# Feed-forward weight rounding moved from the first cross-attention's scores to its keys and values, read from a turned copy

## What is computed

```
# block 1: keys and values of context and latents, 4 kv heads of 96, 16 query heads
hidden = concatenate([context, latents], axis=1)          # 4096 + 256 tokens
k = hidden @ Wk.T ; v = hidden @ Wv.T ; q = latents @ Wq.T
out = softmax(q @ k.T / sqrt(96)) @ v @ Wo.T
# block 6: feed-forward in whole numbers, I = 2752, D = 1024
def _quant_w(W):                       # one scale for each row of W
    ws = maximum(max(abs(W), axis=1, keepdims=True) / 127, 1e-8)
    return clip(round(W / ws), -127, 127), ws
gate = (q @ Wgq.T) * s * wsg.T ; up = (q @ Wuq.T) * s * wsu.T     # Wg, Wu: 2752 x 1024
h = silu(gate) * up ; q2, s2 = _quant_act(h)
out = (q2 @ Wdq.T) * s2 * wsd.T                                   # Wd: 1024 x 2752
```

## Time and profile before

| | |
|---|---|
| median of 3 runs | 2087.39 us (2087.0 to 2088.69) |
| the profiled execution's own time | 2098.17 us |
| its span | 2096.8 us, mean granted TensorE clock 0.962 |
| latent stage, chunks 0 to 16 | 79.1 to 650 us |
| a context chunk of it | 33.9 us |
| cross stage, first score to the first matmul of its output projection | 659.94 to 1094.56 us |
| feed-forward stage | 2003 us to the end |

### The profile page before, as it was taken

How to read it: one execution, slowest core, us unless ns; L and a number is a source line. 1 busy time by engine, 2 the same in 40 slices (tenths; PEclk the granted TensorE clock), 3 DMA queues, 4 the chain that set the end, 5 groups by cost and what they waited for, 6 DMA issues and landing times.

```text
span 2096.8 us, 29638 instructions
## 1 busy us (share of the span) xinstructions
PE 1927.6 (92%) x11932; PEld 1414.5 (67%) x11932; DVE 1292.1 (62%) x1608; ACT 860.1 (41%) x1409; POOL 546.6 (26%) x264
## 2 busy tenths in 40 slices
PE   7899999999997999999998996989999999978977
PEld 5799999999996778787776874623333333366833
DVE  3445454454444788889976755757777774266465
ACT  2211111111113666665664451146777777535421
POOL 0000000000001555564510001046777777410000
PEclk9999999999998999999999998879999999999889
DMA  5543433343326656666625426523434320135052
GB/s 178 169 119 94 126 98 113 99 124 92 86 76 169 212 189 199 189 204 207 223 89 152 161 72 180 112 75 79 99 79 91 87 59 1 41 121 219 1 190 74
DMA packets 154808, 259.30 MB, mean 124 GB/s; under 512 B 36477, under 2 KB 102321, under 8 KB 147505
## 3 DMA queue, kind: packets, MB, share of 16 engines
q1 hardware_dynamic: 154673, 257.42, 41.3%
HBM read 192.39 MB, written 61.76 MB: 121 GB/s over the span
## 4 chain that ended last, share of the span: by engine, by line
PE 81%; DVE 10%; ACT 3%; DMA 2%; issue 2%; SPq 0%; POOL 0%; ACTq 0%; DVEq 0%
PE psum L475 10%; PE psum L1720 7%; PE psum L1737 5%; PE psum L456 4%; PE psum L458 4%; PE psum L457 4%; PE psum L443 3%; PE psum L285 3%; PE psum L286 3%; PE psum L287 3%; PE psum L1753 3%; PE psum L816 3%; DVE top L1913 3%; PE psum L817 3%; PE psum L818 3%; PE psum L831 3%
## 5 line engine op out<-in xcount | busy, mean ns | idle before, releaser
L1913 DVE TENSOR_REDUCE top<-psum 128x4 f32<-128x2048 f32 (+1 forms) x146 | 294.0, 2026 | 103.2 <-PE psum L1701 102.9
L1983 POOL TENSOR_TENSOR added<-probs_f 128x1024 f32<-128x1024 f32 x126 | 299.1, 2376 | 181.5 <-ACT probs_f L1838 133.7
L1838 ACT ACTIVATE probs_f<-psum 128x512 f32<-128x512 f32 x512 | 278.5, 594 | 142.0 <-PE psum L1720 129.7
L608 DVE TENSOR_REDUCE top<-psum 128x2 f32<-128x512 f32 x272 | 186.5, 692 | 198.0 <-PE psum L443 197.8
L907 DVE TENSOR_TENSOR probs_low<-probs,probs_high 128x1024 fp32r<-128x1024 f32 x136 | 197.7, 1458 | 77.7 <-ACT probs L870 77.5
L869 ACT ACTIVATE probs_high<-psum 128x1024 fp32r<-128x1024 f32 x136 | 139.9, 1029 | 164.1 <-PE psum L818 151.6
L1720 PE MATMUL psum<-q_rows,k_rows 97*128 97x512 f32 x512 | 197.7, 462 | 3.1 <-DMA q_rows<-t_high 2.4
L1720 PEld LDWEIGHTS psum<-q_rows,k_rows 97*128 97x128 f32 x512 | 80.9, 191 | 174.1 <-ACT probs_f L1838 159.0
L456 PE MATMUL psum<-c_high,w_high 128*128 128x256 f32 (+1 forms) x672 | 190.7, 284 | 3.2 <-issue 3.2
L457 PE MATMUL psum<-c_low,w_high 128*128 128x256 f32 (+1 forms) x672 | 190.6, 284 | 0.0
L458 PE MATMUL psum<-c_high,w_low 128*128 128x256 f32 (+1 forms) x672 | 190.5, 284 | 0.0
(11 more groups left out here) (359 smaller groups left out, 3820.2 us busy)
## 6 DMA issues: line engine op xcount, KB each, us to landing
wf_rows<-in_ffn_w_dram SPq DMA_DIRECT2D x42, 512.0 KB, 4.4
staged<-in_ctxT_dram SPq DMA_DIRECT2D x32, 512.0 KB, 4.7
k_four<-k_high SPq DMA_DIRECT2D x128, 128.0 KB, 3.4
wf_rows<-in_ffn_w_dram SPq DMA_DIRECT2D x8, 1376.0 KB, 7.9
q_dram<-wf_turned SPq DMA_DIRECT2D x42, 256.0 KB, 2.3
gate_up<-q_dram SPq DMA_DIRECT2D x10, 1024.0 KB, 8.1
value_high<-v_high SPq DMA_DIRECT2D x32, 256.0 KB, 3.7
value_low<-v_low SPq DMA_DIRECT2D x32, 256.0 KB, 4.6
```

The lines of the kernel that those rows point to most:

```text
L608: dve.tensor_reduce(top0[:, r0:r0 + 2, n], psum[:, bank, :].rearrange("p (i n) -> p i n", i=2), AX_X, ALU.max).then_inc(*b.bank_read.up())
L1838: act.activation(probs[:, n % 6, half * BANK:(half + 1) * BANK], psum[:, half, :], ACT.Exp, scale=scale).then_inc(*f.exped.up())
L1913: dve.tensor_reduce(top1[:, first:end, t, chunk], psum[:, MAXIMA + first:MAXIMA + end, :], AX_X, ALU.max).then_inc(*f.max_read.up())
L1983: pool.tensor_tensor(added[pair % 4][:], probs[:, n % 6, :], probs[:, (n + 1) % 6, :], ALU.add).then_inc(*f.added.up())
```

## The change

The rounding leaves the cross stage. It is done in chunks 1 to 15 of the latent stage, in six slots a chunk, 90 in all. A slot is one "find" step and one "settle" step, put between the steps of `chunk_steps` at places that the table `SLOTS` gives.

- The weights are read twice. The row maximum is found from rows as before (68 tiles `wf_rows` of 128 x 1024, three buffers; Wd in three parts). The values that are rounded come from a copy of the weights laid out transposed by the host (`ffn_t0` to `ffn_t2`), in 70 pieces ("pairs") of 128 x 2 x 512, four buffers `turned` (one tile of its own, `staged[2]`, and two halves of `xnT`). So PE turns nothing.
- The inverse scale now varies along the free dimension. SP writes a block's inverses to DRAM (`send_inverses`) and reads them back to all partitions (`load_inverses`). POOL multiplies a piece by them (TENSOR_TENSOR, 128 x 1024), ACT adds 12582912.0 and takes it away again into bf16 (two ACTIVATE of 128 x 1024, `settle`), SP stores the piece (`spill`).
- In slot i the "find" step finds tile i's maximum (DVE) and spills piece i - 18 (SP). The "settle" step rounds piece i - 17 (ACT), loads tile i + 3's rows and piece i - 15 (SP); the piece's buffer was spilled from at the "find" step one and a half slots before. SP waits for `topped`, `rounded` and `spilled` at these places.
- To free room, the low part of the queries is written into chunk 1's `c_high` and `c_low`, sent to DRAM and loaded again before the last chunk; ACT waits for `q_low_sent` before it splits chunk 1. The latents go to DRAM too and come back as a staged chunk. The context uses two `staged` tiles instead of four, and four loads stand ahead of the chunks instead of six.
- The cross stage keeps scores, exponentials, splits, `weigh` and `normalise`. The four unit splits stand at steps 120, 124, 128 and 132.
- The rounded weights lie in DRAM as the feed-forward stage's tiles have them: a partition's part of a chunk is 8 KB in one piece, before it was four of 2 KB. The matmuls of the last chunk (192 columns) take one pass instead of two.

```
+            SLOTS = {("mm", 0, 0, 0): "find", ("mm", 0, 0, 5): "settle", ("mm", 0, 1, 1): "find",
+                     ("mm", 1, 0, 0): "settle", ("mm", 1, 1, 0): "find", ("mm", 2, 0, 0): "settle",
...
             def act_chunk(n, half):
                 high = c_high[n % 2][:, 4 * half:4 * half + 4, :]
+                if n == 1:
+                    act.wait_ge(*b.q_low_sent.at(32))
...
+                def settle(r):
+                    z = width_of(*pairs[r][1:3])
+                    wide = turned[r % 4][:, 0:2 * z]
+                    act.wait_ge(*b.scaled.at(r + 1))
+                    act.activation(wide, wide, ACT.Copy, bias=ROUND).then_inc(*b.shifted.up())
+                    act.wait_ge(*b.shifted.at(r + 1))
+                    act.activation(turned[r % 4].bitcast(BF16)[:, 0:2 * z], wide, ACT.Copy,
+                                   bias=-ROUND).then_inc(*b.rounded.up())
...
+                    if m == 0:
+                        pool.wait_ge(*b.inverse_in.at(16 * (block + 1)))
+                    pool.wait_ge(*wt_in[r % 4].at(16 * (r // 4 + 1)))
+                    pool.tensor_tensor(both, both, inverses[block % 2][:, 0:width].unsqueeze(1).broadcast_to([P, 2, width]),
+                                       ALU.mult).then_inc(*b.scaled.up())
...
+                def load_rows(m):
+                    if m >= 3:
+                        sp.wait_ge(*b.topped.at(m - 2))
...
+                def load_turned(r):
+                    if r >= 4:
+                        sp.wait_ge(*spilled[r % 4].at(16 * (r // 4)))
...
+                    for i, part in enumerate(q_low_parts):
+                        sp.wait_ge(*b.q_split.at(8 * i + 8))
+                        sp.dma_start(q_low_dram[:, i * 8 * T:(i + 1) * 8 * T],
+                                     part[0:HD0, :].bitcast(F32)).then_inc(*b.q_low_sent.up(16))
...
+                        if what == "find":
+                            if 0 <= i - LAG - 1 < len(pairs):
+                                spill(i - LAG - 1)
+                        elif what == "settle":
+                            if i + 3 < len(tops):
+                                load_rows(i + 3)
+                            if i in top_end:
+                                send_inverses(top_end.index(i))
+                            if i - LAG + 2 in pair_start:
+                                load_inverses(pair_start.index(i - LAG + 2))
+                            if 0 <= i - LAG + 2 < len(pairs):
+                                load_turned(i - LAG + 2)
...
-                    for what, m, first, last in quant[n]:
-                        if what == "turn":
-                            turn(m, first, last)
...
-                    if n >= quantised_at and unit < ahead_in_cross:
+                    if n in split_after:
...
-                sp.dma_start(tile[:, 0:whole * KT * P].rearrange("p (i m) -> p i m", i=whole),
-                             q_dram[first:first + whole].rearrange("i p m -> p i m")).then_inc(*flag.up(16))
+                tile = gate_up[i % 2][:, which, 0:KT * width].rearrange("p (k n) -> p k n", n=width)
+                sp.dma_start(tile, q_dram[which, i, :, :, 0:width]).then_inc(*chunk_in[i % 2].up(16))
```

More of the change, by code:

```diff
@@ L677, in sync_program @@
+                for n in some:
                     latents = n == LATENTS
@@ L1070, in sync_program @@
                         m += 1
-                    for what, i, first, last in quant[n]:
-                        if what == "turn" and (last > 16 or i < 2 * FT):
-                            spill(i)
-                        elif what == "settle" and i + 2 < NQ:
-                            load_rows(i + 2)
             gpsimd_program()
```

407 lines of the change are left out of this document (191 added, 216 removed).

## The result

The changed kernel takes 2110.5 us in the median of four runs (2107.1 to 2115.5), the kernel before 2088.0 beside it: a ratio of 1.0105, 95% interval 1.0081 to 1.0130. It is slower by 22 us where 2048 was forecast. A later set on another chip gave 1.0124 (1.0082 to 1.0167). The profiled execution took 2107.1 us for a span of 2105.8.

What follows compares the result with a forecast made beforehand. PE was taken to bound both the latent and cross stages. Terms of -45.5, 0, +3, +5 and -2 us sum to -39.5, giving a span of about 2057 and a time of 2048 us, range 2037 to 2076.

Steps and rivals of the forecast that it cites:

- Term 3: Latent-stage chunks: added DMA traffic nearly fills the queue, 33.4 of 33.9 us a chunk, costing +3 us.
- Term 1: Cross stage: without the rounding it falls from 434.6 to 389.1 us, a gain of 45.5 us.
- Term 2: Latent-stage chunks: compute added to DVE, ACT and POOL fits beside PE's unchanged list, priced at 0.
- rival B: Latent-stage chunks: rounding late on ACT as POOL's multiply or a load comes late; 2062 to 2077 us, chance 0.12.
- Term 4: Chunk 0: ACT waits for sends of the queries' low part, delaying the key copy and PE; +5 us (1 to 8).
- Term 5: Feed-forward stage: larger pieces shorten PE's two waits for `gate_up`; -2 us (0 to -5).
- C: Latent-stage chunks: DMA becomes the bound, turned loads and spills at 226 to 243 GB/s; 2110 (2097) us, chance 0.06.

Runs made afterwards that it cites:

- e1: Changed kernel with each block's inverse scales turned by VectorE and sent as 16 pieces of 128 bytes; 2084.9 us, ratio 0.9948.
- e9: e6 with each slot's turned-tile load put ahead of the row load in SyncE's queue; 2070.2 us, ratio 0.9896.
- e6: e1 with the two sends of the queries' low part issued as early as their data allow; 2082.6 us, ratio 0.9963.
- e10: e1 with half of each row load left out from the fourth on (scales wrong); 2070.8 us (one run).
- e12: e13 with turned tiles loaded three slots ahead instead of two, and rows two instead of three; 2105.9 us, ratio 1.0062.
- e7: e1 plus a send of the inverses in 512 packed 4-byte pieces that nothing reads; 2123.3 us (one run).
- e13: Changed kernel with 16-byte inverse pieces, GpSimd reading factors strided, early send of the queries, turned loads before rows; 2069.1 us, ratio 0.9891.
- e8: e1 plus an unread send of the inverses in 512 4-byte pieces lying 512 bytes apart; 2078.8 us (one run).
- e5: Changed kernel with each block's inverses sent as 128 pieces of 16 bytes, landing in the wrong order; 2074.0 us (one run).

## Why the prediction was wrong

**Term 3 failed.** "12.5 + 8.1 + 12.8 = 33.4 us of 33.9" lists what each slot moves and leaves out what each block moves. A block's scales go out as 2 KB, by bytes nothing; in 4-byte pieces packed into those 2 KB they were 34.5 us of the 58.1 (e1 against the changed kernel), 12 sends of about 3 us each. And they come back to all partitions, which is no longer nothing:

```profile
staged<-inverse_dram SPq DMA_DIRECT2D x12, 256.0 KB, 7.8
```

Eleven of these loads fall into the nine chunks: 2.9 MB, which at the sum's own 370 GB/s are 7.8 us of queue time (an estimate). With them 33.4 us a chunk become about 34.3, above 33.9. The changed code says `allow_slow_non_contiguous` there and the kernel before has no such transfer, so the send was an operation to bound from both sides, and the prediction does not name it.

**The other 23.6 us are this term too**, in its second half: "I take half of the excess". Where the queue is as full as PE, the question is no longer the sum but how late a single load may come. The answer was two slots for turned tiles and 8 to 11 us, while their loads land after medians of 5.8 to 7.2 us even in e1 and a multiply of 2.4 follows. Order gives 5 us of it back (e9's stretch against e6's), halving the rows 10 (e10's against e1's), and lead moved to the turned tiles took away their waits and made new ones (e12). A version with more lead for both streams, which wants another 4 KB of SBUF a partition, was not tried, so how much of the last 13 us would go with lead stays open. The rates were a part of it as well: e1 ran 304 GB/s at a share of 0.93, so 327 when full, where the sum's 11.6 MB in 33.4 us are 346. At 327 they take 35.4 us, 1.5 more than the chunk has, an estimated 12 to 13 us over 8.5 chunks; the 10 us that halving the rows brought agree. The 13 us that stay in e10 have another reason, since there the share was 0.88; that it is lateness is argued from the waits of GpSimd and ScalarE, and no run removes all of them at once.

Could the added work of VectorE, ScalarE and GpSimd be the reason, without any late load? A chunk of e9 with all three streams keeps the old pace, so that work fits beside PE's list where the loads are in time (columns as above):

```profile
290.84:324.69 33.85, 32.80 (x250) 32.37 (x249) 24.72 (x32) 16.83 (x20) 12.40 (x6) 1.00 0.98 321
```

Four of e9's nine chunks do so (33.8 to 33.9 us).

**Term 1 was right:** 389.0 us for a forecast of 389.1. Steps follow each other in 2.77 us, the boundary waits for the sums are 5.6 us (5.5 before), the wait for `probs_low` 5.0 on the weight loads. These are groups and waits of the changed kernel from 732 to 1106 us:

```profile
L1046 DVE TENSOR_TENSOR probs_low<-probs,probs_high 128x1024 fp32r<-128x1024 f32 x133 | 162.8, 1225 | 200.2 <-ACT probs L1012 200.2
...
PE psum L992 <- DVE sums L329: 5.6, 6, 1.4
PEld psum L992 <- DVE probs_low L1046: 5.0, 3, 1.8
```

The subtraction fell from 1458 ns to 1225, next to the 1222 of the earlier trace rows, now that GpSimd has nothing to do there.

**Term 2** was right where it could be seen: chunks 1 to 3, with maxima alone, and 13 to 15, with settles at most, keep 33.7 us each. One thing it did not have: VectorE's subtraction of the context is slower where GpSimd multiplies beside it. Before it took 1222 ns; in the changed kernel (minimum, median, maximum)

```profile
L562 DVE TENSOR_TENSOR c_low<-staged,c_high x34: 1211/1225/3426, 63.3 to 658.3; 128x1024 fp32r<-128x1024 f32 x34
```

A chunk's two subtractions take 2.36 us where no multiply overlaps them, and 6.71 at 382.71 us, with multiplies at 382.70 and 385.90 that keep their own length (2.35 and 2.44 us). So VectorE loses nearly a multiply each time, as the last sentences of rival B have it; but from 231 to 600 us the mean of one is 2.09 us, so in this stage it is not few that collide. It hardly costs PE time by itself: in the chunk of e9 above the pair took 4.81 us, and the chunk lasted 33.85.

**Term 4** was right in its mechanism and too small: 7.2 us, and 2 more in the next chunk, where 5 was taken and 8 was the bound. ScalarE was released at 91.9 for a forecast of 88.9. The rate was not what failed: from 83 to 87 and from 87 to 92 us the engines moved 311 and 341 GB/s, better than the 226 that was taken. But that is 2.9 MB, and the two sends have 1.6: a context load was ahead of them, and the latents' store, issued at 82.5 us behind the second send, went out beside them.

**Term 5:** -2.2 us for -2. PE's wait for `gate_up`, 4.3 us before, is now 2.1.

**The check on the profiled span.** The prediction took 10.8 us off because the profiled execution of before lay that much above its median. The edit-free stretch shows those 10.3 us. The profiled execution of after lies 3.4 below its median, so spans may not be compared without this.

Of the rivals, C gave 2097 to 2110 us and the slower side, and had the right place. That it names the measured time is luck: its price came from slow bytes in the turned loads and spills; the cause was few bytes in small pieces, plus lateness and a queue somewhat overfull. B's chain (GpSimd late, ScalarE late, the first copy late) is what carried it to PE, in all nine chunks and not by GpSimd's own slowness.

## What to carry to other kernels

List a change's transfers by instruction, not by bytes: one with a turned access pattern deserves a line of its own, and so does one that spreads a small buffer over all partitions, above all in a queue that is planned to be full. If small values must be turned on their way to DRAM, keep each partition's values together and let the reader stride, or turn them on an engine first. When a queue is as full as the bound engine, a forecast has to compare each load's lead with its landing time under load; and a queue's order puts first what has the least lead.

## What the runs showed of the hardware

- 512 stores of 4 bytes into one range of 2 KB hold up the transfers around them: 133 GB/s in the mean from 6 to 12 us behind their issue (105 in e7), against 286 to 301 at the same distance in the runs without them, with a share near 1.0 in the 5 us windows shown. The same stores 512 bytes apart do not, nor do 128 stores of 16 bytes into the same 2 KB, nor 16 of 128 bytes.
- The packed stores cost nothing in the end where the queue has room: chunks 1 to 3 of the changed kernel have two such sends and keep 33.7 us.
- GpSimd's multiply of 128 x 1024 takes 3.01 us in the mean with its second input read at a stride of 16 bytes (e13), 2.43 with it in sequence (the changed kernel).
- A VectorE subtraction of 128 x 1024 with both inputs in SBUF takes 1222 ns alone, and up to 3426 where a GpSimd multiply runs beside it; the multiply is not slowed (2.35 and 2.44 us).
- Open: from the output projection's first matmul to GpSimd's first sum (L2020), where these kernels do the same work, the six profiled runs with e1's edit (e1, e6, e7, e8, e9, e10) took 283 to 290 us, the nine without it 276 to 278, and the kernel before 282. So something that goes with e1's edit costs some 7 us or more far behind the stage that it changes, and no run here shows what; e5, with e1's stretch, is 11 us faster than e1. It is as large as several effects argued about here; hence the stretch as a measure beside the time.
